# The second layer's normalised x turned by sixteen block transposes of VectorE instead of four of TensorE

## The chip, the core and the metric

The kernel runs on one core of one Trainium2 chip. What counts is the device time of one execution in microseconds, as the median of several runs. The engines are called by the names of the profile: PE (TensorE), ACT (ScalarE), DVE (VectorE), POOL (GpSimd) and SP (SyncE, which here only issues DMAs). Each engine works through its own queue in order.

## What is computed

Two layers over 8 sequences of 512 tokens with 128 features, all in fp32. Each layer adds an attention and a feed-forward part to x, both fed by the same layer norm of x:

```python
xn = _layernorm(x, axis=-1)
x = x + _L0_attn_ref(xn, ...) + _L0_ffn_ref(xn, ...)
xn = _layernorm(x, axis=-1)
x = x + _L1_attn_ref(xn, L1_attn_w_qkv, L1_attn_w_proj) + _L1_ffn_ref(xn, k0, k1, k2, s0, s1, s2)
```

The first layer's attention has 16 heads with two softmax maps each (differential attention); its feed-forward part is one product with x and the weights rounded in blocks of 32. The second layer's attention has 16 heads of 8 features with a rotary embedding. Its feed-forward part is three products with weights of +1 and -1 (128 to 512 to 512 to 128) with relu between them. So in the second layer xn feeds q, k and v, and the first feed-forward product.

## The kernel before

A sequence lies in x_all with its tokens on the 128 partitions, four per partition (T = 4), and 128 features behind each. Attention is computed in 24 units (ORDER): A and B are the two halves of the first layer's maps of a sequence, C is the second layer of one. A unit has 16 steps (STEPS). In each step PE makes four tiles of scores (`scores`, line 858), ACT takes their exponentials in two instructions (line 707), and PE multiplies the exponentials of two steps before with the values (`pv`, line 877). Between these, each step carries the jobs that the tables FIRST, LOOP and LAST list by hand for that unit and step: the norms, projections and feed-forward products of other sequences. LOOP is run for b = 2 to 5. Every engine walks through the same tables and does its own part of each item, so that a table's order is the order of all queues. A job of PE writes the one PSUM tile ps_misc, and DVE or ACT takes it out (TAKER); the next job waits for that.

The items around the change, for a sequence b:

- `norm1` parts 0 to 4 (`layer_norm`): DVE computes the layer norm of x; its last instruction (line 988) writes xn, with tokens on partitions.
- `x_t1`: PE waits for that, transposes four 128x128 tiles of xn into ps_misc (line 721), and DVE copies the result to xn_t (line 1135), which has features on partitions and the tokens in the free dimension, tile by tile (column 128 t + p). For b = 1 to 5 it is in step 14 of a unit C, and the norm's last part in step 12 (b = 1) or 13. In b = 0 and 6 it is in step 12, in b = 7 in step 11; there a `regroup` (DVE, lines 1318 and 1320) lies between norm and x_t1.
- `split_xn` (POOL): waits until xn_t has been taken, then rounds it to xn_hi (line 615) and computes xn_lo = xn_t - xn_hi (line 617).
- `ff0`, f = 0 to 3: PE waits for the split and multiplies xn_hi and xn_lo with the first feed-forward weights (lines 732 and 733); ACT applies the relu (line 657) and DVE splits the result (lines 1104 and 1106). The first comes in the step 0 of the unit after x_t1 for b = 1 to 5, two steps after x_t1 for b = 0 and 6, and four steps after it for b = 7.
- `q1`, `k1`, `v1`: PE waits for xn_t and multiplies it with the weights (line 728). q1 comes one step after x_t1 for b = 0, 6 and 7. For b = 1 to 4 it comes five steps after it and for b = 5 four, behind ff0.
- `take` (line 1308): DVE takes the products of eight steps out of ps_pv with block transposes; a following `pv` waits for it.

xn_hi and xn_lo lie in a part of the tiles of the second feed-forward stage (h1_hi, h1_lo), which `ff2_b` of the sequence before reads.

Of the kernel before, what the change touches and what calls it, by code (L numbers as in the profile page):

```python
# [18 lines left out]
T = N // P  # L19
# [39 lines left out]

TAKER = dict(x_t0="dve", x_t1="dve", q0="dve", k0="dve", v0="dve", q1="dve", k1="dve", v1="dve",  # L60
             qk_norm1="dve", w_t="dve", quant_t="dve", quant_mm="dve",
# [37 lines left out]
     15: [("ff_t", 0)]},  # L99
# [16 lines left out]
     9: [("take", -1, "C", 0), ("regroup", -1, "C", 0), ("project0", 0), ("norm1", 0, 0)], 11: [("norm1", 0, 1), ("norm1", 0, 2)],  # L116
     13: [("norm1", 0, 3), ("norm1", 0, 4)], 14: [("x_t1", 0)]},
]
# [99 lines left out]
def two_layers(nc, x_in, w_qkv0, w_proj0, b_proj0, lq1, lk1, lq2, lk2, subln, w_ffn0, b_ffn0,  # L218
               w_qkv1, w_proj1, k0, k1, k2, s0, s1, s2, rope, out):
    with ExitStack() as ctx:  # L220
# [21 lines left out]
        xn = sb("xn", [P, T, D], F32)  # L242
# [82 lines left out]
        first_written = [sem("first_written_q"), sem("first_written_k")]  # L325
        parts_written = [[sem(f"parts_written{layer}_{i}") for i in "qk"] for layer in range(2)]
        xn_split = sem("xn_split")
        ff_split = sem("ff_split")
# [121 lines left out]
        def load_shift(eng, U, half=None):  # L450
# [6 lines left out]
            for i in range(PARTS):  # L457
                if half is None:
                    eng.dma_start(q[ROWS[layer] + i::TILE_ROWS[layer], slot:slot + n].bitcast(F32),
                                  shift[h0:h0 + H, i, :].bitcast(F32)).then_inc(shift_loaded[U.stack], 16)  # L460
                    continue
                for g in range(TILES[layer]):
                    r, h = TILE_ROWS[layer] * g + ROWS[layer] + i, n * g + n // 2 * half
                    eng.dma_start(q[r:r + 1, n // 2 * half:n // 2 * (half + 1)].bitcast(F32),
                                  shift[h:h + n // 2, i, :].bitcast(F32)).then_inc(shift_loaded[group(U, half)], 16)

        def unit(kind, b):
# [114 lines left out]
        def _(pool):  # L582
# [28 lines left out]
            def split_xn(b):  # L611

                wait_taken(pool, ("x_t1", b))
                own_instruction(pool)
# [16 lines left out]
            def run(items):  # L631
                for name, b, *_ in items:
                    if name == "v_move":
                        move_values(b)
                    elif name == "x_t1":
                        split_xn(b)
# [81 lines left out]
        def _(pe):  # L718
# [16 lines left out]
            def job(item):  # L735
# [11 lines left out]
                if name == "w_t":  # L747
                    pe.wait_ge(setup_ops, SETUP_OPS - 2)
                    pe.wait_ge(quant_ops, 2 * QUANT_OPS)
                    ins = nc.tensor.transpose(ps[:, 0:P], quant[:, 0:P], ident[:])  # L750
                elif name in ("x_t0", "x_t1"):
                    pe.wait_ge(norm_ops[layer], (b + 1) * LN_OPS)
                    if item == ("x_t0", 0):

# [10 lines left out]
                elif name in ("q0", "k0", "q1", "k1"):  # L765
                    after("x_t" + name[1], b)
                    if item == ("q0", 0):
# [3 lines left out]
                elif name in ("v0", "v1"):  # L771
                    after("x_t" + name[1], b)
                    w = (w0_v if layer == 0 else w1_v)[:]
# [160 lines left out]
        def _(dve):  # L934
# [174 lines left out]
            def job(item):  # L1109
# [21 lines left out]
                elif item == ("x_t0", 0):  # L1131

                    taken(nc.vector.tensor_copy(xn_t[:, 0:N // 2], ps[:, 0:N // 2]))
                elif name in ("x_t0", "x_t1"):
                    taken(nc.vector.tensor_copy(xn_t[:], ps))  # L1135
# [168 lines left out]
            def take_pair(b, kind, pr):  # L1304
# [4 lines left out]
                last[:] = pv_taken, 2 * u + pr + 1  # L1309

            def regroup(b, kind, pr):

# [80 lines left out]
            def run(items):  # L1393
                for item in items:
# [20 lines left out]
                    elif name == "regroup":  # L1415
                        regroup(b, *args)
                    elif name in ("out_t0", "out_t1"):
                        turn_out(int(name[-1]), b)
# [62 lines left out]
```

## Time and profile before

| | us |
|---|---|
| median of 3 runs | 874.63 |
| lowest and highest | 871.47 and 875.64 |
| the profiled execution | 872.51 |
| its span, from first to last instruction | 870.7 |

All numbers of the trace are of that one execution. Busy times of an engine are the union of its instructions' times. In the timeline an instruction's row may stand for several like ones in a row (x4), and square brackets give how long the engine had been idle before it and which instruction ended that. Mean granted clock of TensorE over the span is 0.98 of full speed.

### The profile page before, as it was taken

Reading aid. Unit: us, or ns where it says so; the run is one execution under the profiler, and the core shown is the slowest. Engines: PE = TensorE matmul, PEld = TensorE weight load, DVE = VectorE, ACT = ScalarE, POOL = GpSimd, SP = SyncE. Lnnn points to the kernel's source line nnn. Section 1 sums busy time; section 2 is a strip of 40 time slices with the busy share of each in tenths; the row PEclk is TensorE's granted clock in tenths of the full one; section 3 lists DMA queues with packets and bytes.
Section 4 is the critical chain, followed back from the end, with each engine's and each line's share of the span. In section 5 each row is a group of like instructions: output and inputs, shape, how many; then the busy total and the mean of one; then the engine's idle time right before and its main releaser. Section 6 shows DMA issues by size and latency. Waiting matters only on the chain.

```text
span 870.7 us, 17841 instructions
## 1 busy us (share of the span) xinstructions
PE 808.3 (93%) x6767; PEld 287.7 (33%) x6767; DVE 545.4 (63%) x1205; ACT 765.2 (88%) x856; POOL 36.0 (4%) x57
## 2 busy tenths in 40 slices
PE   6688898999999989999999999999998999999995
PEld 4122222342333323333233323333242323333342
DVE  6667478676774666746775567756677476476321
ACT  3679997889889998999889998999988999889984
POOL 5000000000000000000000000000000000000000
PEclk9889998999999999999999999999999999999998
DMA  6807315630728015460527407281164704205100
GB/s 182 170 9 149 52 50 148 146 49 8 209 49 142 11 69 142 104 99 1 148 62 142 59 1 209 50 138 16 49 162 100 102 17 133 52 1 167 43 13 13
DMA packets 41618, 75.52 MB, mean 87 GB/s; under 512 B 5872, under 2 KB 7024, under 8 KB 41520
## 3 DMA queue, kind: packets, MB, share of 16 engines
q1 hardware_dynamic: 39612, 68.45, 36.1%
q0 software_dynamic: 1824, 5.70, 2.1%
q8 instruction: 57, 0.93, 0.5%
q14 instruction: 33, 0.27, 0.1%
q10 hardware_dynamic: 92, 0.16, 0.1%
HBM read 36.84 MB, written 35.65 MB: 83 GB/s over the span
## 4 chain that ended last, share of the span: by engine, by line
PE 72%; ACT 11%; DVE 9%; issue 5%; DMA 1%; DVEq 0%; SPq 0%; ACTq 0%; POOL 0%; POOLq 0%
PE ps_pv L877 31%; PE ps_s L858 20%; ACT probs L707 11%; PE ps_misc L728 7%; PE ps_misc L732 7%; PE ps_misc L733 5%; PE ps_misc L721 2%; DMA q_ab<-shift 1%; DVE pv_sb L1308 1%; DVE v_aug L1167 1%; DVE tmp L1159 0%; DVE h_lo L1106 0%; DVE tmp L1158 0%; PE ps_misc L779 0%; ACT ff_out L657 0%
## 5 line engine op out<-in xcount | busy, mean ns | idle before, releaser
L707 ACT ACTIVATE probs<-ps_s 128x1024 f32<-128x1024 f32 x768 | 726.5, 1046 | 61.8 <-PE ps_s L858 60.5
L877 PE MATMUL ps_pv<-probs,v_aug 128*32 128x512 f32 x3072 | 413.5, 610 | 10.2 <-ACT probs L707 5.8
L858 PE MATMUL ps_s<-q_ab,k_ab 18*128 18x512 f32 (+1 forms) x1088 | 143.5, 500 | 28.8 <-ACT probs L707 20.3
L858 PEld LDWEIGHTS ps_s<-q_ab,k_ab 18*128 18x128 f32 (+1 forms) x1088 | 54.7, 184 | 197.7 <-ACT probs L707 153.7
L877 PEld LDWEIGHTS ps_pv<-probs,v_aug 128*32 128x32 f32 x3072 | 61.9, 108 | 118.5 <-issue 81.2
L732 PE MATMUL ps_misc<-h_hi,k_w 128*128 128x512 f32 x192 | 85.7, 446 | 2.7 <-DVE v_aug L1167 1.2
L858 PE MATMUL ps_s<-q_c,k_c 34*128 34x512 f32 x448 | 84.8, 453 | 0.0
L1104 DVE CAST h_hi<-ff_out 128x512 fp32r<-128x512 f32 x64 | 27.4, 428 | 89.0 <-ACT ff_out L657 87.5
L1308 DVE STREAM_TRANSPOSE pv_sb<-ps_pv 128x512 f32<-128x512 f32 x48 | 34.4, 717 | 70.8 <-PE ps_pv L877 67.5
L733 PE MATMUL ps_misc<-h_lo,k_w 128*128 128x512 f32 x192 | 75.9, 395 | 0.0
L732 PEld LDWEIGHTS ps_misc<-h_hi,k_w 128*128 128x128 f32 x192 | 35.9, 187 | 88.4 <-issue 48.8
L858 PEld LDWEIGHTS ps_s<-q_c,k_c 34*128 34x128 f32 x448 | 36.1, 184 | 74.7 <-ACT probs L707 60.2
L657 ACT ACTIVATE ff_out<-ps_misc 128x512 f32<-128x512 f32 x64 | 39.1, 610 | 17.9 <-PE ps_misc L733 13.8
L1106 DVE TENSOR_TENSOR h_lo<-ff_out,h_hi 128x512 fp32r<-128x512 f32 x64 | 44.3, 692 | 2.2
L733 PEld LDWEIGHTS ps_misc<-h_lo,k_w 128*128 128x128 f32 x192 | 36.1, 188 | 4.3
L1191 DVE TENSOR_TENSOR x_all<-ps_misc,x_all 128x512 f32<-128x512 f32 x24 | 16.6, 692 | 26.3 <-PE ps_misc L721 12.8
L728 PE MATMUL ps_misc<-xn_t,w_qk 128*32 128x512 f32 x248 | 32.3, 592 | 0.0
L1167 DVE COPY v_aug<-ps_misc 128x512 f32<-128x512 f32 x14 | 9.7, 692 | 27.5 <-PE ps_misc L728 27.1
L615 POOL CAST h_hi<-xn_t 128x512 fp32r<-128x512 f32 x8 | 4.9, 608 | 502.9 <-DVE xn_t L1135 502.9
L1320 DVE TENSOR_TENSOR heads<-pv_sb,recip 128x256 f32<-128x256 f32 x48 | 20.4, 425 | 1.7
L728 PE MATMUL ps_misc<-wp,quant_t 128*32 128x128 f32 x512 | 17.8, 282 | 2.7 <-DVE quant_t L1327 2.7
L728 PEld LDWEIGHTS ps_misc<-wp,quant_t 128*32 128x32 f32 x512 | 15.2, 113 | 12.8 <-issue 11.3
(164 smaller groups left out, 563.1 us busy)
## 6 DMA issues: line engine op xcount, KB each, us to landing
parts_dram<-qk_parts SPq DMA_DIRECT2D x32, 512.0 KB, 3.7
parts_dram<-qk_parts SPq DMA_DIRECT2D x62, 256.0 KB, 4.1
q_ab<-parts_dram SPq DMA_DIRECT2D x60, 128.0 KB, 4.6
k_ab<-parts_dram SPq DMA_DIRECT2D x60, 128.0 KB, 5.9
q_c<-parts_dram SPq DMA_DIRECT2D x14, 512.0 KB, 7.5
k_c<-parts_dram SPq DMA_DIRECT2D x14, 512.0 KB, 8.8
out_dram<-x_all POOLq DMA_DIRECT2D x8, 256.0 KB, 6.8
x_all<-in_L_attn_x_dram POOLq DMA_DIRECT2D x7, 256.0 KB, 6.1
```

Source lines behind the costliest of these rows:

```text
L657: nc.scalar.activation(ff_out[:], ps_misc[:], ACT.Relu).then_inc(job_taken_act, 1)
L707: nc.scalar.activation(probs[:, U.slot(s), 2 * half:2 * half + 2], ps_s[:, 2 * pair:2 * pair + 2], ACT.Exp, scale=SCALE[U.layer]).then_inc ...
L728: ins = nc.tensor.matmul(ps[c, :], w[:, c], x, start=True, stop=True)
L732: nc.tensor.matmul(ps, w, hi, start=start, stop=False)
L733: return nc.tensor.matmul(ps, w, lo, start=False, stop=stop)
L858: ins = nc.tensor.matmul(ps_s[:, bank, :], k[row:row + n, slot, c * P:(c + 1) * P], q[row:row + n, slot, :], start=True, stop=True)
L877: ins = nc.tensor.matmul(ps_pv[32 * j:32 * j + 32, :], v_aug[:, U.v, c, a:a + 32], probs[:, U.slot(s), j, :], start=c == 0 and not odd, st ...
L1104: nc.vector.tensor_copy(hi, ff_out[:]).then_inc(ff_split, 1)
L1106: nc.vector.tensor_tensor(lo, ff_out[:], hi.bitcast(F32), ALU.subtract).then_inc(ff_split, 1)
L1167: taken(nc.vector.tensor_copy(own_values(unit("C" if layer else "A", b).v), ps.rearrange("p (t h e) -> p t h e", t=T, h=H)))
L1308: nc.vector.transpose(pv_sb[:], ps_pv[:]).then_inc(pv_taken, 1)
L1320: nc.vector.tensor_tensor(dst, v[:, :, :, 0:HD], rows(recip[:], HD), ALU.mult).then_inc(regroup_ops, 1)
```

## The change

The job x_t1 goes. In its place in the tables stand the two parts of `turn1`. In each part DVE issues eight block transposes. Each takes 32 of xn's partitions (tokens), all four t and 32 features: four blocks of 32x32, which it turns and writes to the 32 rows of xn_t that belong to these features. A source of 32 partitions a is written to four targets f, so that sixteen instructions fill xn_t. Each increments a new semaphore, turned[1]; the readers of xn_t in PE (q1, k1, v1) and in POOL (split_xn) wait for its count of 16 per sequence. split_xn now also waits for ff2_b of the sequence before, which the queue of jobs had implied. PE has no part in the turning any more, and ps_misc isn't used for it. The first layer's x is turned as before (x_t0). The diff, without two of the tables' hunks that read like the others:

```diff
@@ -57,7 +57,7 @@
 INDEX = {unit: u for u, unit in enumerate(ORDER)}
 
 
-TAKER = dict(x_t0="dve", x_t1="dve", q0="dve", k0="dve", v0="dve", q1="dve", k1="dve", v1="dve",
+TAKER = dict(x_t0="dve", q0="dve", k0="dve", v0="dve", q1="dve", k1="dve", v1="dve",
              qk_norm1="dve", w_t="dve", quant_t="dve", quant_mm="dve",
              project0="dve", project1="dve", ff0="act", ff1="act", ff1_b="act", ff2="act", ff2_b="act", ff_t="dve",
              fast="dve")
@@ -84,7 +84,7 @@
     {1: [("take", 0, "B", 1), ("regroup", 0, "B", 1), ("combine", 0, 0)], 3: [("combine", 0, 1), ("combine", 0, 2)],
      4: [("combine", 0, 3)], 5: [("combine", 0, 4), ("combine", 0, 5)], 6: [("out_t0", 0), ("project0", 0), ("norm1", 0, 0)],
      8: [("norm1", 0, 1)], 9: [("take", 1, "A", 0), ("norm1", 0, 2), ("norm1", 0, 3)], 11: [("norm1", 0, 4), ("regroup", 1, "A", 0)],
-     12: [("x_t1", 0)], 13: [("q1", 0)], 14: [("rope", 0, "q", 0), ("ff0", 0, 0)], 15: [("rope", 0, "q", 1), ("k1", 0)]},
+     12: [("turn1", 0, 0), ("turn1", 0, 1)], 13: [("q1", 0)], 14: [("rope", 0, "q", 0), ("ff0", 0, 0)], 15: [("rope", 0, "q", 1), ("k1", 0)]},
     {0: [("take", 1, "A", 1), ("rope", 0, "k", 0)], 2: [("rope", 0, "k", 1), ("ff0", 0, 1)],
      3: [("qk_norm1", 0), ("norm0", 2, 0), ("norm0", 2, 1)], 4: [("v1", 0)], 5: [("exact1", 0)],
      6: [("ff0", 0, 2), ("norm0", 2, 2), ("ff0", 0, 3)], 7: [("norm0", 2, 3)], 8: [("norm0", 2, 4), ("x_t0", 2)],
@@ -95,7 +95,7 @@
      3: [("quant_t", 2), ("bias", 2), ("combine", 1, 0), ("combine", 1, 1), ("combine", 1, 2)], 4: [("quant_mm", 2)],
      5: [("combine", 1, 3)], 6: [("ff1", 0, 3), ("combine", 1, 4), ("ff1_b", 0, 3)], 7: [("exact0", 2), ("combine", 1, 5)],
      8: [("v0", 2)], 9: [("take", 0, "C", 0), ("out_t0", 1)], 10: [("regroup", 0, "C", 0), ("project0", 1), ("norm1", 1, 0)],
-     11: [("norm1", 1, 1), ("norm1", 1, 2), ("norm1", 1, 3)], 12: [("norm1", 1, 4), ("ff2", 0), ("ff2_b", 0)], 14: [("x_t1", 1)],
+     11: [("norm1", 1, 1), ("norm1", 1, 2), ("norm1", 1, 3)], 12: [("norm1", 1, 4), ("ff2", 0), ("ff2_b", 0)], 14: [("turn1", 1, 0), ("turn1", 1, 1)],
      15: [("ff_t", 0)]},
 ]
 
@@ -114,7 +114,7 @@
     {1: [("take", 0, "B", 1), ("ff_t", -1)], 2: [("regroup", 0, "B", 1)], 3: [("combine", 0, 0)], 4: [("v0", 1), ("combine", 0, 1)],
      5: [("combine", 0, 2), ("combine", 0, 3)], 7: [("combine", 0, 4), ("combine", 0, 5)], 8: [("out_t0", 0)],
      9: [("take", -1, "C", 0), ("regroup", -1, "C", 0), ("project0", 0), ("norm1", 0, 0)], 11: [("norm1", 0, 1), ("norm1", 0, 2)],
-     13: [("norm1", 0, 3), ("norm1", 0, 4)], 14: [("x_t1", 0)]},
+     13: [("norm1", 0, 3), ("norm1", 0, 4)], 14: [("turn1", 0, 0), ("turn1", 0, 1)]},
 ]
 
 LAST = [
...
...
@@ -324,6 +324,7 @@
         bound0_ops = sem("bound0_ops")
         first_written = [sem("first_written_q"), sem("first_written_k")]
         parts_written = [[sem(f"parts_written{layer}_{i}") for i in "qk"] for layer in range(2)]
+        turned = [sem("turned0"), sem("turned1")]
         xn_split = sem("xn_split")
         ff_split = sem("ff_split")
         v_moved = sem("v_moved")
@@ -464,6 +465,13 @@
                     eng.dma_start(q[r:r + 1, n // 2 * half:n // 2 * (half + 1)].bitcast(F32),
                                   shift[h:h + n // 2, i, :].bitcast(F32)).then_inc(shift_loaded[group(U, half)], 16)
 
+        def wait_turned(eng, layer, b):
+
+            if layer == 0:
+                wait_taken(eng, ("x_t0", b))
+            else:
+                eng.wait_ge(turned[layer], 16 * (b + layer))
+
         def unit(kind, b):
             return Unit(INDEX[kind, b])
 
@@ -610,7 +618,10 @@
 
             def split_xn(b):
 
-                wait_taken(pool, ("x_t1", b))
+                wait_turned(pool, 1, b)
+                if b > 0:
+
+                    wait_taken(pool, ("ff2_b", b - 1))
                 own_instruction(pool)
                 nc.gpsimd.tensor_copy(xn_hi, xn_t[:]).then_inc(xn_split, 1)
                 pool.wait_ge(xn_split, 2 * b + 1)
@@ -629,10 +640,10 @@
                 nc.gpsimd.tensor_copy(own_values(unit("C", b).v), x_all[:, b - 5].rearrange("p t (h e) -> p t h e", h=H)).then_inc(v_moved, 1)
 
             def run(items):
-                for name, b, *_ in items:
+                for name, b, *args in items:
                     if name == "v_move":
                         move_values(b)
-                    elif name == "x_t1":
+                    elif name == "turn1" and args[0] == 1:
                         split_xn(b)
                     elif name == "project1":
                         store(b)
@@ -748,9 +759,9 @@
                     pe.wait_ge(setup_ops, SETUP_OPS - 2)
                     pe.wait_ge(quant_ops, 2 * QUANT_OPS)
                     ins = nc.tensor.transpose(ps[:, 0:P], quant[:, 0:P], ident[:])
-                elif name in ("x_t0", "x_t1"):
-                    pe.wait_ge(norm_ops[layer], (b + 1) * LN_OPS)
-                    if item == ("x_t0", 0):
+                elif name == "x_t0":
+                    pe.wait_ge(norm_ops[0], (b + 1) * LN_OPS)
+                    if b == 0:
 
                         for t in range(T):
                             ins = nc.tensor.transpose((ps if t < T // 2 else ps_s[:, 1, :])[:, t * P:(t + 1) * P], xn[:, t, :], ident[:])
@@ -763,13 +774,13 @@
                     pe.wait_ge(fast_w_made, n + 1)
                     ins = in_columns(ps, fast_w[:, n * P:(n + 1) * P], xn_t[:])
                 elif name in ("q0", "k0", "q1", "k1"):
-                    after("x_t" + name[1], b)
+                    wait_turned(pe, layer, b)
                     if item == ("q0", 0):
                         pe.wait_ge(w0_made, 4)
                     w = (w0_qk if layer == 0 else w1_qk)[:, 0 if name[0] == "q" else 1, :]
                     ins = in_columns(ps, w, xn_t[:])
                 elif name in ("v0", "v1"):
-                    after("x_t" + name[1], b)
+                    wait_turned(pe, layer, b)
                     w = (w0_v if layer == 0 else w1_v)[:]
                     for t in range(T):
                         ins = in_columns(ps[:, t * P:(t + 1) * P], xn_t[:, t * P:(t + 1) * P], w)
@@ -1131,7 +1142,7 @@
                 elif item == ("x_t0", 0):
 
                     taken(nc.vector.tensor_copy(xn_t[:, 0:N // 2], ps[:, 0:N // 2]))
-                elif name in ("x_t0", "x_t1"):
+                elif name == "x_t0":
                     taken(nc.vector.tensor_copy(xn_t[:], ps))
                 elif name == "quant_t":
                     taken(nc.vector.tensor_copy(quant_t[:], ps))
@@ -1308,6 +1319,15 @@
                 nc.vector.transpose(pv_sb[:], ps_pv[:]).then_inc(pv_taken, 1)
                 last[:] = pv_taken, 2 * u + pr + 1
 
+            def turn(layer, b, part):
+
+                settled()
+                for a in (2 * part, 2 * part + 1):
+                    for f in range(4):
+                        dst = xn_t[32 * f:32 * f + 32].rearrange("p (t a c) -> p a t c", t=T, a=4)[:, a]
+                        nc.vector.transpose(dst, xn[32 * a:32 * a + 32, :, 32 * f:32 * f + 32]).then_inc(turned[layer], 1)
+                last[:] = turned[layer], 16 * (b + layer - 1) + 8 * (part + 1)
+
             def regroup(b, kind, pr):
 
                 G = 2 * INDEX[kind, b] + pr
@@ -1414,6 +1434,8 @@
                         take_pair(b, *args)
                     elif name == "regroup":
                         regroup(b, *args)
+                    elif name in ("turn0", "turn1"):
+                        turn(int(name[-1]), b, *args)
                     elif name in ("out_t0", "out_t1"):
                         turn_out(int(name[-1]), b)
                     elif name == "bound0":
```

## Rows read from the trace of the kernel before

**Rows 1.** The page, part 1: span, and busy time of the engines
```profile
span 870.7 us, 17841 instructions
...
PE 808.3 (93%) x6767; PEld 287.7 (33%) x6767; DVE 545.4 (63%) x1205; ACT 765.2 (88%) x856; POOL 36.0 (4%) x57
```

**Rows 2.** Groups by line and form, DVE: busy us, mean ns | idle before
```profile
L1327 DVE STREAM_TRANSPOSE quant_t<-heads 128x512 f32<-128x512 f32 x8 | 5.7, 712 | 0.3
L1327 DVE STREAM_TRANSPOSE quant_t<-quant 128x512 f32<-128x512 f32 x8 | 5.7, 711 | 0.3
...
L1179 DVE STREAM_TRANSPOSE norm_row<-norm_ok 32x32 f32<-32x32 f32 x8 | 1.6, 199 | 0.4 <-DVE norm_ok L1177 0.2
```

**Rows 3.** Timeline of DVE: start us, us, instruction; dependent pair, then independent pair
```profile
196.01 0.16 DVE L952 TENSOR_TENSOR stat<-stat 128x4 f32<-128x4 f32 x1
196.20 0.16 DVE L954 SCALAR_TENSOR_TENSOR stat<-stat 128x4 f32<-128x4 f32 x1
...
32.10 0.28 DVE L1363 TENSOR_TENSOR bias<-bias 128x128 f32<-128x128 f32 x1
32.30 0.28 DVE L1364 TENSOR_SCALAR wp<-wp,sub_col 128x128 f32<-128x128 f32 x1
```

**Rows 4.** Timeline of all engines around the turn of b = 2
```profile
301.42 0.69 DVE L988 TENSOR_TENSOR xn<-tmp,stat 128x512 f32<-128x512 f32 x1
...
302.63 0.66 PE L721 MATMUL ps_misc<-ident,xn 128*128 128x128 f32 x4
...
303.32 0.69 DVE L1135 COPY xn_t<-ps_misc 128x512 f32<-128x512 f32 x1 [1.21 <-PE ps_misc L721]
...
304.88 1.27 POOL L617 TENSOR_TENSOR h_lo<-xn_t,h_hi 128x512 fp32r<-128x512 f32 x1
...
306.42 0.50 PE L732 MATMUL ps_misc<-h_hi,k_w 128*128 128x512 f32 x1
306.75 0.40 PE L733 MATMUL ps_misc<-h_lo,k_w 128*128 128x512 f32 x1
...
307.45 0.63 ACT L657 ACTIVATE ff_out<-ps_misc 128x512 f32<-128x512 f32 x1
```

**Rows 5.** Busy time: stretch, us, PE, PEld, DVE, ACT, POOL, clock, DMA
```profile
294.70:314.00 19.30, 18.63 (x138) 5.56 (x136) 11.07 (x29) 19.30 (x22) 1.88 (x2) 1.00 0.01 1
```

**Rows 6.** Timeline at b = 1, 0, 6 and 7: last work before, first reader
```profile
197.86 0.69 DVE L988 TENSOR_TENSOR xn<-tmp,stat 128x512 f32<-128x512 f32 x1
...
204.20 0.50 PE L732 MATMUL ps_misc<-h_hi,k_w 128*128 128x512 f32 x1
...
116.77 0.43 DVE L1320 TENSOR_TENSOR heads<-pv_sb,recip 128x256 f32<-128x256 f32 x1
...
119.92 1.04 PE L728 MATMUL ps_misc<-xn_t,w_qk 128*32 128x512 f32 x8
...
709.69 0.43 DVE L1320 TENSOR_TENSOR heads<-pv_sb,recip 128x256 f32<-128x256 f32 x1
...
711.29 1.04 PE L728 MATMUL ps_misc<-xn_t,w_qk 128*32 128x512 f32 x8
...
778.14 0.42 DVE L1320 TENSOR_TENSOR heads<-pv_sb,recip 128x256 f32<-128x256 f32 x1
...
780.74 1.04 PE L728 MATMUL ps_misc<-xn_t,w_qk 128*32 128x512 f32 x8
```

**Rows 7.** Timeline of PE at two stalls; busy time (as Rows 5) behind them
```profile
140.05 0.50 PE L732 MATMUL ps_misc<-h_hi,k_w 128*128 128x512 f32 x1 [1.16 <-DVE v_aug L1167]
...
671.19 1.77 PE L877 MATMUL ps_pv<-probs,v_aug 128*32 128x512 f32 x8 [1.93 <-DVE pv_sb L1308]
...
671.42:674.83 3.41, 3.41 (x20) 0.69 (x16) 0.43 (x2) 1.07 (x3) 0.00 (x0) 0.50 0.94 235
142.35:149.17 6.82, 6.59 (x32) 1.70 (x28) 4.96 (x17) 4.37 (x5) 0.00 (x0) 0.50 0.50 108
```

4 rows, old and new, of the table LAST are left out of this document.

## The prediction

> **What bounds the kernel now.** I read the page first [rows 1]: TensorE (PE) is busy 808.3 of 870.7 us, ScalarE (ACT) 765.2, VectorE (DVE) 545.4. So two engines are nearly full, and VectorE has room on average. That average is not what decides here: all queues are in order, and what counts is when a result of VectorE is wanted by TensorE. The second view is the groups of instructions by line [rows 2], with prices of block transposes. The third is the timeline around the eight places where the second layer's x is turned, one for each sequence b; a unit there is sixteen steps, and in each step TensorE makes the scores, then the products of the step before last, then the jobs of the table. The fourth is the busy time by stretches, which shows the granted clock.
>
> At b = 2 [rows 4] the timeline reads: the layer norm's last instruction (L988) ends at 302.11. TensorE comes to the four transposes at 302.63, VectorE copies xn_t at 303.32 to 304.01, GpSimd (POOL) ends its split of it at 304.88 + 1.27 = 306.15, and TensorE reads the split in the first ff0 matmul at 306.42, in the middle of a queue without a gap. From the end of the norm to that read are 4.31 us, of which GpSimd takes 2.14 from the end of the copy to the end of its split. So VectorE has 302.11 to about 304.1 to deliver xn_t, 2.0 us, before TensorE has to stand still. b = 3, 4 and 5 repeat this pattern.
>
> **What goes.** Per sequence four transposes, and one copy of 0.69 us. The four transposes are one merged row of 0.66 us [rows 4], so TensorE gets back at most 8 x 0.66 = 5.3 us in all. I cost it at zero in b = 2 to 5: ScalarE is busy in 19.30 of the 19.30 us from 294.7 to 314.0 [rows 5], so a TensorE that is 0.66 us earlier meets a ScalarE that is not. In b = 0, 1, 6, 7 it would be worth up to 0.66 us each, if TensorE did not then wait for xn_t; below it does, so the gain is swallowed there as well.
>
> **What comes.** Sixteen STREAM_TRANSPOSE instructions of 32 partitions x 128 elements, one behind the other with no wait between those of one part. No row of before has this form. One alone is bounded well: 32x32 elements take 199 ns and 128x512 take 711 ns [rows 2], a slope of (711 - 199) / 480 = 1.07 ns per element, so 128 elements take 199 + 96 x 1.07 = 301 ns. The period is what is unknown:
> - Upper end, as if each waited for the one before: small dependent instructions start 0.19 to 0.20 us apart at 0.16 us each (L952, L954), some 0.035 us beyond the duration [rows 3]. Period 0.336, sixteen take 5.4 us.
> - Lower end, as independent instructions of 128 elements do: L1363 and L1364 start 0.20 us apart, though each lasts 0.28 [rows 3]. Fifteen periods of 0.20 and one duration, 3.3 us.
> - Far end, elements alone with nothing between them: 15 x 128 x 1.07 ns + 0.30 = 2.4 us.
>
> I take 5.4 us. The rows that overlap all stay on partitions 0 to 127 from one instruction to the next; here every instruction writes another group of 32 partitions than the one in front of it, and the nearest row in form, the 32x32 block transpose of 199 ns, is followed by nothing that overlaps it. The Trainium skill, page "VectorE: DVE Perf Modes", section "Two Vector instructions with no wait between them", says it as a rule: an instruction whose output starts in another quadrant than the last output is held until every earlier one has finished. By that rule all sixteen are held and the sum is the one at 5.4 us; without it, the one at 3.3 us. No row of before tells which. The same page of the Trainium skill, section "Rules for kernel authors", sends a whole 128x128 transpose to TensorE where PSUM will do as its target, which speaks against this change; no row of before compares the two.
>
> **Who waits.** The copy ends after one further instruction; now xn_t is ready 5.4 us after VectorE is free. At each site the first reader in TensorE's queue stands still, and behind it stand scores and products; ScalarE then runs dry.
> - b = 2: 302.11 + 5.4 = 307.5; GpSimd ends 2.14 later, 309.65; ff0 starts at 309.7 for 306.42, TensorE 3.3 late. ScalarE's relu came at 307.45 [rows 4]; it can't start before the job's second matmul ends, 306.75 + 0.40 - 306.42 = 0.73 us after ff0's start, so at 310.45. ScalarE is 3.0 late. Both engines being late, I charge 3.0. Four such: 12.0.
> - b = 1: norm ends 198.55, xn_t at 203.95, split at 206.1; ff0 for 204.20 at 206.15, TensorE 1.95 late. ScalarE takes some 0.3 of it as above; charge 1.7 [rows 6].
> - b = 0: here a regroup (L1320, ends 117.19) lies between norm and turn, and q1 follows one step on. xn_t at 122.6, q1 for 119.92 at 122.7: 2.8. The split is then ready before ff0 [rows 6].
> - b = 6: regroup ends 710.12, xn_t 715.5, q1 for 711.29 at 715.6: 4.3. b = 7: 778.56, 784.0, 784.05 for 780.74: 3.3 [rows 6].
>
> Sum 12.0 + 1.7 + 2.8 + 4.3 + 3.3 = 24.1 us. VectorE's own addition, 8 x (5.4 - 0.7) = 38 us, costs nothing beyond this: its next work at b = 2 is the split of the relu's result (L1104), and the relu came at 307.45 [rows 4], about when the turn ends. GpSimd's two new waits are for the turn itself and for ff2_b of the sequence before, long done in the table; behind them its queue holds only stores and value moves. SyncE's loads shift with the rope results, by no more than all else.
>
> **What the stalls do to the clock.** TensorE idles 1.93 us before 671.19, and from 671.42 to 674.83 it is granted 0.50, the 1.2 GHz level, while busy all the 3.41 us [rows 7]; half of its work of that time, 1.7 us, is lost. An idle time of 1.16 us before 140.05 is followed by 6.82 us at 0.50 from 142.35 [rows 7]. The eight new stalls are 1.9 to 4.3 us, at or above those that the low level followed. Some of the low stretch may lie in the stall itself. I charge 1.5 us each, 12 us; the ends are 0 and 2.5 each.
>
> **Sum.** 872.5 (the profiled execution, span 870.7) + 24.1 + 12 = 908.6 us. The median of the three runs is 2.1 us above the profiled one; I say 908.
>
> **Rivals.**
> 1. The instructions overlap, 3.3 us per turn. Stalls: b = 2 to 5 1.0 each at ScalarE (split ends 302.11 + 3.3 + 2.14 = 307.55, relu at 308.4), b = 0 0.7, b = 1 none, b = 6 2.2, b = 7 1.2: 8.1 us, and the low clock behind one or two of them, 1.6 to 3. Time 882 to 884. For it: L1363/L1364. Against: they don't change partitions.
> 2. Turns as in the forecast, but the stalls leave the clock alone, since they fall differently: 872.5 + 24.1 = 896.6, or 892 to 900. Against it: the two places above, with idle times no longer than these.
> 3. The other side: short turns. At 2.4 us only b = 6 and 7 stall (1.3, 0.3), b = 0 and 1 gain as much; no change. From 2.0 us per turn downward nothing waits in b = 2 to 5, and TensorE's 0.66 us count in b = 0, 1, 6, 7 at most: 4 x 0.66 = 2.6 us faster, 870. It needs a period of 0.11 us, below the 128 elements of 1.07 ns.
> 4. The change doesn't take TensorE's part away: excluded by the diff, since no job x_t1 is left.
>
> **How the numbers follow.** Forecast with low clock 0.62, rival 2 0.13, rival 1 0.16, rival 3 0.04 faster and 0.04 no change, 0.01 else. The forecast's own range is 900 to 917 (stalls 22 to 27 us by a turn of 5.1 to 5.8, clock 5 to 18). Including rival 2 and most of rival 1 gives 882 to 917. A measurement of this kernel tells about 0.5%, 4.4 us, from no change; rivals 1 and 2 lie above it. So faster 0.04, same 0.05, slower 0.91.
>
> **What would show it.** Right: sixteen rows of about 0.30 us in each turn, 0.33 to 0.34 apart, GpSimd's L615 waiting for them, ff0 waiting for GpSimd by about 3 us at b = 2 to 5 and q1 waiting for the turn at b = 0, 6, 7; the granted clock at 0.5 behind these. Wrong: periods near 0.20 (rival 1), TensorE waits of 3 us with a clock that stays (rival 2), or first reads that find xn_t ready (rival 3). The forecast fails most easily in the period of the transposes and in what a stall costs beyond its own length.

## The result: 5.7% slower, and what the profile after shows

The changed kernel takes 923.17 us (median of 4 runs, 916.92 to 926.62), the kernel before 873.86 us in the runs beside it; the ratio is 1.0567, 95% interval 1.0522 to 1.0611. The forecast was 908 us with a range of 882 to 917. The direction was right, the size was not: +49 us measured, +34 us forecast. The profiled execution took 923.29 us, its span is 921.5 us, and the mean granted clock of TensorE over it is 0.947, where it was 0.98.

From the page after, the lines that answer to [rows 1], and two groups of part 5 (line, engine, operation, busy us, mean ns of one, idle before and what ended it):

```profile
span 921.5 us, 17881 instructions
...
PE 831.1 (90%) x6735; PEld 288.6 (31%) x6735; DVE 578.6 (63%) x1325; ACT 767.4 (83%) x856; POOL 35.8 (4%) x57
...
L1328 DVE STREAM_TRANSPOSE xn_t<-xn 32x128 f32<-32x128 f32 x128 | 38.7, 303 | 4.1
L626 POOL CAST h_hi<-xn_t 128x512 fp32r<-128x512 f32 x8 | 4.9, 607 | 534.6 <-DVE xn_t L1328 534.6
```

A page read by busy shares alone would mislead here: DVE's share is 63% before and after, although it has 33 us more to do, and PE is *busier*, 831.1 for 808.3 us, although 32 transposes have gone. PE has more busy time with less work because it spends more of it at the lower clock, as the stretches below and the run with filled waits show.

The waits of PE (who waited for whom, us in total, times, longest) name the new stalls:

```profile
PE ps_misc L743 <- POOL h_lo L628: 15.9, 5, 3.5
PE ps_misc L739 <- DVE xn_t L1328: 11.0, 3, 4.5
PE ps_s L869 <- DMA q_ab<-shift: 9.5, 2, 7.1
```

The first is ff0 waiting for the split at b = 1 to 5, the second q1 waiting for the turn at b = 0, 6 and 7: 26.9 us. The forecast had PE late by 1.95 + 4 x 3.3 = 15.2 us at the first and 10.4 us at the second, 25.6 together. The timeline at b = 2 answers to [rows 4]:

```profile
310.07 0.69 DVE L999 TENSOR_TENSOR xn<-tmp,stat 128x512 f32<-128x512 f32 x1
...
310.80 5.32 DVE L1328 STREAM_TRANSPOSE xn_t<-xn 32x128 f32<-32x128 f32 x16
...
317.00 1.25 POOL L628 TENSOR_TENSOR h_lo<-xn_t,h_hi 128x512 fp32r<-128x512 f32 x1
318.41 0.58 PE L743 MATMUL ps_misc<-h_hi,k_w 128*128 128x512 f32 x1 [3.29 <-POOL h_lo L628]
...
319.45 0.60 ACT L668 ACTIVATE ff_out<-ps_misc 128x512 f32<-128x512 f32 x1 [3.23 <-PE ps_misc L744]
320.07 1.94 PE L888 MATMUL ps_pv<-probs,v_aug 128*32 128x512 f32 x8
```

Sixteen transposes take 5.32 us, (5.32 - 0.30) / 15 = 0.335 us from start to start; ff0 stands 3.29 us. All of that is as forecast. The last line is what was not priced in full: a group of products takes 1.94 us where it takes 1.06 to 1.07 us at full clock. The busy time by stretches shows the low level (1.2 GHz, 0.50) behind each of the eight stalls; here are b = 2 and 3, which differ (columns as in [rows 5]):

```profile
318.62:322.03 3.41, 3.41 (x15) 0.64 (x14) 1.12 (x2) 2.39 (x3) 0.00 (x0) 0.50 0.01 2
424.43:434.67 10.24, 9.86 (x40) 2.68 (x44) 3.74 (x7) 6.57 (x8) 0.23 (x1) 0.50 0.01 2
```

The low stretches at the eight turns last 3.41 us at b = 0, 1 and 2, 10.24 us at b = 3, 4, 5 and 7, and 6.83 us at b = 6: 58 us in all. PE is busy in 55 of them, at half speed, so some 28 us of its work are lost there by this estimate. The charge had been 1.5 us each, 12 in all.

### The profile page after: what moved, and what is told of

The parts are those of the page before. It is cut to its first block, busy times and chain, and to the rows that moved or that the text cites. A ratio compares the mean times of both kernels' runs of the same rounds, so it can differ in the third digit from the quotient of the medians.

```text
span 921.5 us, 17881 instructions
## 1 busy us (share of the span) xinstructions
PE 831.1 (90%) x6735; PEld 288.6 (31%) x6735; DVE 578.6 (63%) x1325; ACT 767.4 (83%) x856; POOL 35.8 (4%) x57
## 4 chain that ended last, share of the span: by engine, by line
PE 64%; DVE 17%; ACT 9%; issue 5%; DMA 2%; POOL 1%; SPq 1%; DVEq 0%; ACTq 0%; POOLq 0%
PE ps_pv L888 28%; PE ps_s L869 17%; ACT probs L718 8%; PE ps_misc L739 7%; PE ps_misc L743 7%; PE ps_misc L744 5%; DVE xn_t L1328 4%; PE ps_misc L732 1%; DMA q_ab<-shift 1%; DVE pv_sb L1319 1%; DVE tmp L990 1%; POOL h_lo L628 1%; DVE xn L999 1%; DVE stat L992 1%; DVE stat L963 1%
## 5 line engine op out<-in xcount | busy, mean ns | idle before, releaser
L888 PE MATMUL ps_pv<-probs,v_aug 128*32 128x512 f32 x3072 | 426.9, 629 | 7.7 <-ACT probs L718 3.8
L869 PE MATMUL ps_s<-q_ab,k_ab 18*128 18x512 f32 (+1 forms) x1088 | 148.2, 518 | 32.4 <-ACT probs L718 22.7
L743 PE MATMUL ps_misc<-h_hi,k_w 128*128 128x512 f32 x192 | 88.7, 462 | 18.1 <-POOL h_lo L628 15.9
L744 PE MATMUL ps_misc<-h_lo,k_w 128*128 128x512 f32 x192 | 78.5, 409 | 0.0
L739 PE MATMUL ps_misc<-xn_t,w_qk 128*32 128x512 f32 x248 | 36.6, 666 | 11.0 <-DVE xn_t L1328 11.0
L1328 DVE STREAM_TRANSPOSE xn_t<-xn 32x128 f32<-32x128 f32 x128 | 38.7, 303 | 4.1
L1202 DVE TENSOR_TENSOR x_all<-ps_misc,x_all 128x512 f32<-128x512 f32 x24 | 16.6, 692 | 24.1 <-PE ps_misc L739 11.3
L1169 DVE TENSOR_TENSOR tmp<-ps_misc,trig 128x512 f32<-128x512 f32 x16 | 11.1, 692 | 21.8 <-PE ps_misc L739 21.2
```

Source lines behind the costliest of these rows:

```text
L739: ins = nc.tensor.matmul(ps[c, :], w[:, c], x, start=True, stop=True)
L743: nc.tensor.matmul(ps, w, hi, start=start, stop=False)
L744: return nc.tensor.matmul(ps, w, lo, start=False, stop=stop)
L869: ins = nc.tensor.matmul(ps_s[:, bank, :], k[row:row + n, slot, c * P:(c + 1) * P], q[row:row + n, slot, :], start=True, stop=True)
L888: ins = nc.tensor.matmul(ps_pv[32 * j:32 * j + 32, :], v_aug[:, U.v, c, a:a + 32], probs[:, U.slot(s), j, :], start=c == 0 and not odd, st ...
L1328: nc.vector.transpose(dst, xn[32 * a:32 * a + 32, :, 32 * f:32 * f + 32]).then_inc(turned[layer], 1)
```

## Experiments

Three questions were open: does the period of 0.335 us come from the change of partitions, are the stalls the whole of the loss or does something else add to it, and what is DVE's turn worth where nobody waits for it. All ratios are to the kernel before, run beside each. A trace is of one execution, and where its time isn't the run's median, the text says so.

**Same group of partitions.** Each transpose writes to the group of 32 partitions that it reads, so that xn_t is then not the transposed x:

```diff
-                        dst = xn_t[32 * f:32 * f + 32].rearrange("p (t a c) -> p a t c", t=T, a=4)[:, a]
+                        dst = xn_t[32 * a:32 * a + 32].rearrange("p (t a c) -> p a t c", t=T, a=4)[:, f]
```

> The sixteen transposes of a turn read the same elements as in the changed kernel, but each writes the 32 rows of xn_t that carry the same partition numbers as its source, in another block of columns. So xn_t is not the transposed x, and the second layer computes with wrong operands; sizes and instructions are the same. Four transposes in a row keep source and target partitions. Theory (an instruction waits for the earlier ones when it changes its group of 32 partitions): starts within a group of four 0.20 us apart, 0.34 between groups, a turn of 3.8 us in place of 5.4; waits of PE at the eight turns fall from 26.9 us to about 14, and the time lands at 895 to 905. Rival (block transposes never overlap, whatever they touch): starts stay 0.34 apart, the time stays at 917 to 927.

Measured in one run: 894.7 us. The turn at b = 2, in the timeline of DVE:

```profile
308.00 3.63 DVE L1328 STREAM_TRANSPOSE xn_t<-xn 32x128 f32<-32x128 f32 x16
```

3.63 us in place of 5.32. In a group of four the starts are 0.235, 0.193 and 0.193 us apart, and 0.29 where the group changes; the median transpose shows 260 ns in place of 303. So block transposes do overlap when they stay on their partitions, and the rival falls. PE waits 7.5 + 6.0 = 13.5 us at the turns, about 14 had been expected; the time is just below the 895 to 905 expected.

**Targets kept, sources changed.** The turn as in the changed kernel, with the loops exchanged:

```diff
-                for a in (2 * part, 2 * part + 1):
-                    for f in range(4):
+                for f in (2 * part, 2 * part + 1):
+                    for a in range(4):
```

> The same sixteen transposes in another order: the target group is the outer loop, so that four in a row write the same 32 partitions and only the source group changes. Theory (a change of the source's group holds an instruction as well as one of the target's): starts stay 0.34 apart, turn 5.4 us, time 917 to 927. Rival (only a change of the target's group holds it): twelve of sixteen starts are 0.20 apart, turn 3.8 us, time 895 to 905.

Measured: 924.5 us in one run, and the same turn as in the changed kernel:

```profile
310.24 5.31 DVE L1328 STREAM_TRANSPOSE xn_t<-xn 32x128 f32<-32x128 f32 x16
```

Keeping the target alone brings nothing: with the source's group changed, each instruction starts 0.33 us or more behind the one before, whose own time is 0.30 us. A turn by whole 32-partition pieces can't avoid both, since each pair of source and target occurs once.

**The waits filled with matmuls.** The useless work goes into PE's queue ahead of the wait, so that PE waits as long for the same thing but doesn't stand still (and likewise ahead of q1 for b = 0, 6 and 7):

```diff
+FILLERS = (3, 2, 3, 3, 3, 3, 4, 4)
...
+                    if f == 0 and b in (1, 2, 3, 4, 5):
+                        for _ in range(FILLERS[b]):
+                            in_columns(ps, wp1[:], trig[:, 0, :])
                     pe.wait_ge(xn_split, 2 * (b + 1))
```

> The changed kernel, with matmuls of no use (fp32, four of 32 columns by 512, about 0.9 us a group) put into PE's queue ahead of each of the eight waits: three groups at b = 0, 2, 3, 4, 5, two at b = 1, four at b = 6 and 7. The waits keep their end, PE does not stand still. Theory (the 22 to 25 us that the change costs beyond the waits themselves are PE at half clock behind them): granted clock back to 0.98, time 923 - 22 = 898 to 903. Rival (the rest comes from somewhere else, such as later results of DVE): the time stays within 3 us of 923, or grows by what the fillers take.

Measured: 898.35 us (4 runs), ratio 1.0293 (1.024 to 1.0347), mean granted clock 0.982. Timeline at b = 2, then the busy time of the 10.24 us behind the wait at b = 3:

```profile
311.35 2.76 PE L740 MATMUL ps_misc<-trig,wp 128*32 128x512 f32 x24
...
314.74 0.50 PE L744 MATMUL ps_misc<-h_hi,k_w 128*128 128x512 f32 x1 [0.63 <-POOL h_lo L629]
...
315.84 1.06 PE L895 MATMUL ps_pv<-probs,v_aug 128*32 128x512 f32 x8
...
419.80:430.04 10.24, 9.86 (x74) 2.92 (x74) 6.70 (x13) 9.28 (x12) 0.00 (x0) 1.00 0.01 2
```

ff0 comes as late behind the norm as in the changed kernel without fillers (7.6 us behind its end in both), but the clock is 1.00 behind it and the products take 1.06 us. This run splits the loss. By the medians 898.4 - 873.9 = 24.5 us (25.6 by the ratio) are the stalls themselves, for which the forecast was 24.1 us, and the 923.2 - 898.4 = 24.8 us that come back with the fillers are the rest. The four runs spread from 896.3 to 903.9, and the interval of the ratio leaves 21 to 30 us for the stalls and 19 to 28 for the rest.

The starts of ACT's exponentials, compared step by step between the profiled executions (872.5, 896.6 and 923.3 us), say where the two parts lie. The stalls add 24.4 us at the eight turns in the filled kernel. Without the fillers another 26.7 us are lost, all of it at these places to 0.2 us:

| Place | low stretch, us | lost beyond the filled kernel, us |
|---|---|---|
| b = 0, 1, 2 | 3.41 each | 1.5, 0.8, 1.3 |
| b = 6 | 6.83 | 2.7 |
| b = 3, 4, 5, 7 | 10.24 each | 4.0, 3.9, 4.2, 4.0 |
| start of unit A of b = 7 | 6.83, behind a DMA wait | 2.9 |
| the first units, ahead of any turn | | 1.5 |

So some 22.5 us are the clock behind the eight stalls. The other 4.4 us come back with the fillers too, but not at the turns.

**DVE's part alone.** The kernel before with the sixteen transposes added ahead of its own copy:

```diff
+                if name == "x_t1":
+                    settled()
+                    for a in range(4):
+                        for f in range(4):
+                            dst = xn_t[32 * f:32 * f + 32].rearrange("p (t a c) -> p a t c", t=T, a=4)[:, a]
+                            nc.vector.transpose(dst, xn[32 * a:32 * a + 32, :, 32 * f:32 * f + 32]).then_inc(turned, 1)
+                    last[:] = turned, 16 * (b + 1)
                 dve.wait_ge(job_made, PLAN.made[item])
```

> The kernel before with the sixteen transposes of DVE added ahead of its own copy of xn_t: PE still transposes, DVE's copy overwrites the turned x with the same values. Readers wait for the copy. This does DVE's part alone. Theory (only the time at which xn_t is ready counts): each wait of PE is that of the changed kernel plus 0.73 us for the copy, 26.9 + 8 x 0.73 = 32.7 us, and as much clock loss behind them: 923 + 6 = 929, 925 to 934. Rival (PE's part gone, and not DVE's length, is what lets the clock fall and the kernel slow down): below 900.

Measured: 928.61 us (4 runs), ratio 1.0647 (1.0613 to 1.0681). With PE's transposes in place the kernel loses what the changed one loses, and a little more for the copy, 5.4 us for the 6 expected. PE waits 16.5 us for POOL at b = 2 to 5, 12.2 us for DVE at b = 0, 6 and 7, and at b = 1 2.5 us one job earlier, at the transposes of the feed-forward result, which follow in ps_misc: 31.2 us for the 32.7 expected. The trace is of the fastest of the four executions, 923.22 us at a clock of 0.959; the other three took 928.5 to 932.3 at 0.944 to 0.946. The loss is in the time at which xn_t is ready, and not in TensorE's missing part.

**TensorE's part gone, at next to no price.** Two of a turn's sixteen transposes; fourteen of the sixteen blocks of xn_t are left out:

```diff
-                for a in (2 * part, 2 * part + 1):
-                    for f in range(4):
+                for a in (2 * part,):
+                    for f in (0,):
...
-                        nc.vector.transpose(dst, xn[...]).then_inc(turned[layer], 1)
+                        nc.vector.transpose(dst, xn[...]).then_inc(turned[layer], 8)
```

> The changed kernel with one transpose per part in place of eight, so two of the sixteen of a turn; fourteen of the sixteen blocks of xn_t keep an older sequence's values, and the second layer computes with them. All else runs as in the changed kernel. This leaves PE's part gone and takes DVE's price away: the turn takes 0.7 us. Theory: nothing waits, granted clock 0.98, and since ACT sets the pace around the turns of b = 2 to 5 only b = 0, 1, 6 and 7 may gain, up to 0.6 each: 870.5 to 874. Rival (PE bounds everywhere, as its 93% busy says): 8 x 0.66 = 5 us, 868 to 869.

Measured: 871.97 us (12 runs), ratio 0.9982 (0.9964 to 1.0000), so 1.6 us won, with an interval that just reaches no change, of at most 5.3 us that TensorE no longer spends. In b = 2 to 5 PE begins the scores behind the transposes 0.6 us earlier than in the kernel before, and is back at the old place one step on: ACT sets the pace there, as [rows 5] said. Even a turn at next to no price would have brought 0.2%.

**Readers later.** First for b = 1 to 5 alone, in the changed kernel and in the kernel before:

```diff
-    {0: [("ff0", -1, 0)], 1: [("take", -2, "C", 1), ("ff0", -1, 1)], 2: [("regroup", -2, "C", 1)], 3: [("q1", -1)],
-     4: [("rope", -1, "q", 0), ("ff0", -1, 2)], 5: [("out_t1", -2), ("rope", -1, "q", 1)], 6: [("k1", -1)],
-     7: [("rope", -1, "k", 0), ("rope", -1, "k", 1)], 9:
+    {1: [("take", -2, "C", 1)], 2: [("regroup", -2, "C", 1), ("ff0", -1, 0)], 3: [("q1", -1)],
+     4: [("rope", -1, "q", 0), ("ff0", -1, 1)], 5: [("out_t1", -2), ("rope", -1, "q", 1)], 6: [("k1", -1)],
+     7: [("rope", -1, "k", 0), ("rope", -1, "k", 1), ("ff0", -1, 2)], 9:
...
```

For b = 5 the table LAST is changed likewise; there q1, k1 and their rotations move by a step too.

> The changed kernel, with ff0 0, 1 and 2 of b = 1 to 5 two to three steps later in the tables (steps 2, 4 and 7 of the A unit in place of 0, 1 and 4), so that the split is ready when PE comes to it. Theory (stall and clock behind it are the whole cost): waits of PE for POOL go from 15.9 us to 0, the five places give back what the step times show there, 3.6 + 4.3 + 7.0 + 7.0 + 7.2 = 29 us, so the time is about 894, 890 to 899, with 11 us of waits left at b = 0, 6 and 7. Rival (DVE's added 38 us weigh on their own): less than half of that comes back, over 908.

> Control for the run before: the kernel before, turned by PE, with the same later ff0 0, 1 and 2 for b = 1 to 5. If the move of these jobs has a price or a gain of its own, it shows here. Theory: PE and ACT are both full in this stretch, the jobs only change places; 872 to 878 us. If it is below 870, the gain found by moving them in the changed kernel was partly the move's own.

Measured: 891.98 us for the changed kernel (4 runs, ratio 1.0200, 1.0164 to 1.0236) and 876.02 us for the one before (10 runs, ratio 1.0031, 1.0015 to 1.0047). The wait of PE for POOL is gone, and with it 31 of the 49 us. In the traces the changed kernel is 3.2 us behind the other at the start of unit A of b = 2, and 3.1 us behind it at step 10 of unit B of b = 6: the turns of b = 2 to 5 between them, and b = 1's first reader, now cost nothing. What is left between the two, 16.0 us, lies mainly at b = 0, 6 and 7, where q1 still waits:

```profile
PE ps_misc L739 <- DVE xn_t L1328: 11.0, 3, 4.5
```

Then all eight, with q1 and its followers two to three steps later for b = 0, 6 and 7; here b = 6 in the control:

```diff
-     13: [("q1", 6)], 14: [("rope", 6, "q", 0), ("rope", 6, "q", 1), ("ff0", 6, 0)], 15: [("k1", 6)]},
-    {0: [("take", 7, "A", 1), ("regroup", 7, "A", 1)], 1: [("v1", 6)], 2: [("rope", 6, "k", 0), ("ff0", 6, 1)],
+     15: [("q1", 6)]},
+    {0: [("take", 7, "A", 1), ("regroup", 7, "A", 1), ("rope", 6, "q", 0), ("ff0", 6, 0)], 1: [("rope", 6, "q", 1), ("k1", 6)],
+     2: [("rope", 6, "k", 0), ("ff0", 6, 1)], 3: [("v1", 6)],
```

> The changed kernel with every first reader moved behind the turn: ff0 of b = 1 to 5 as in the run before, and q1 with its followers two steps later for b = 7, two to three for b = 0 and 6. Theory (the waits and the clock behind them are the whole cost, DVE's 38 us are free): PE waits 0 to 1 us at the eight turns, granted clock 0.98, the time 892 less 4.2 + 7.0 + 7.3 from the step times there = 873, 868 to 877; and a gain of up to 0.66 us per sequence from PE's part gone, if anywhere, would bring it to 868. Rival: DVE's longer way delays its later work, and the time stays over 880.

> Control: the kernel before with the tables of the run with all readers later. Theory: 872 to 878. The difference to that run is what the turn by DVE costs or brings where nobody waits for it; I expect the run by DVE to be 0 to 3 us faster, since PE is free of 8 x 0.66 us and in most places ACT sets the pace.

Measured: 892.27 us (5 runs, ratio 1.0216) and 892.66 us for the control (5 runs, ratio 1.0221). The 873 us of the expectation were missed by 19 us, and the control shows why: my table has a price of its own. Of the control's waits of PE, and in its timeline the k1 of b = 6 and the ff0 behind it:

```profile
PE ps_misc L734 <- DVE tmp L1161: 12.1, 7, 5.3
```

```profile
730.75 1.04 PE L730 MATMUL ps_misc<-xn_t,w_qk 128*32 128x512 f32 x8
...
738.56 0.80 PE L734 MATMUL ps_misc<-h_hi,k_w 128*128 128x512 f32 x1 [5.34 <-DVE tmp L1161]
```

At b = 0 and 6 I had put the second ff0 one step behind k1, whose result DVE takes only after other work, and PE stands before that ff0 for 4.5 and 5.3 us. The comparison still answers its question for b = 1 to 5: from the start of unit A of b = 2 to step 10 of unit B of b = 6 the distance between the two traces stays at 1.3 to 1.4 us. There nobody waits for the sixteen transposes, and DVE's longer work costs nothing and brings nothing. That the whole times agree to 0.4 us proves less: the control has a DMA wait of 3.85 us at the start of unit A of b = 7 that the other run lacks, and at b = 0 and 6 both stand still for other reasons.

**TensorE's old waits filled.** The kernel before, with fillers at five of its own waits, and then at three:

```diff
+            def fill(ps, n):
+                for _ in range(n):
+                    in_columns(ps, ident, xn[:].rearrange("p t d -> p (t d)"))
...
                         if s == 0:
+                            fill(ps_s[:, 0, :], 6)
                             wait_taken(pe, ("fast", 0, "k", 0))
```

> The kernel before, untouched but for matmuls of no use in PE's own five long waits: six groups (about 0.9 us each) before the first scores, four before the first transposes of quant, one before ff0 2 of b = 0, two before the ninth product step of unit B of b = 6, two before the last projection. Theory (a wait of PE costs half of its work for some time behind it, wherever it comes from): the low stretches behind 24.3, 44.8, 140, 671 and 862.5 go; 1.5 + 1.5 + 2.4 + 1.6 + 0.9 = 8 us, time 864 to 870, granted clock above 0.99. Rival (the clock falls for another reason than PE standing still, such as the DMAs running then): clock and time stay.

> The kernel before with the useless matmuls at three of the five places only: seven groups before the first scores, four before the first transposes of quant, two before the last projection. The place in unit B of b = 6 is left as it was, since in the run with all five the loads of the next unit came late there and took back 4.8 us. Theory: the 2.5 us won in the first unit and 0.9 us in the last stay, 874 - 3 = 871, 869 to 872. Rival (what PE wins early is always lost at that load again): 873 to 877.

With five: 876.89 us (9 runs), ratio 1.0044 (1.0026 to 1.0062), where 864 to 870 had been expected. With three (seven groups in place of six at the first): 871.69 us (12 runs), ratio 0.9981 (0.9967 to 0.9995), as expected. With five the median clock is 0.987, above the 0.98 of the kernel before, and the kernel is still slower, so a higher mean clock is not in itself time won. The traced execution is the best of the nine: 873.22 us at a clock of 0.994, the time of the kernel before; the other eight took 876.2 to 878.8 at 0.984 to 0.989, and no trace shows where their clock fell. In the traced one no low stretch is left at the first four places, which speaks for PE's standing still as what the clock fell for, and PE is 3.2 us ahead up to unit B of b = 6. Then the loads for unit A of b = 7 have not landed when PE comes to them, and a longer wait of PE with the low level behind it takes back 4.8 us. The same scores in the kernel before, and in this run:

```profile
684.31 0.51 PE L858 MATMUL ps_s<-q_ab,k_ab 18*128 18x512 f32 x4 [0.49 <-DMA q_ab<-shift]
```

```profile
683.15 0.80 PE L864 MATMUL ps_s<-q_ab,k_ab 18*128 18x512 f32 x4 [4.15 <-DMA q_ab<-shift]
```

The kernel before waits there too, but for 0.49 us; its low stretch of [rows 7] lay ahead of the same loads. The loads don't keep pace with PE: from the first of the DMAs issued ahead of these scores to the scores 15.6 us pass in the kernel before and 17.6 us here. The run with three fillers leaves that place alone and is 0.2% faster than the kernel before. It isn't a clean test of that place, since it leaves out the filler at b = 0 as well, and the filler at b = 6 also brings a wait for ps_misc with it.

## Why the forecast had the right sign and the wrong size

- **What bounds the kernel, and that b = 2 to 5 gain nothing from TensorE's part**: right. At next to no price for DVE the whole gain is 1.8 us by the medians; the bound in rival 3 was 2.6 us.
- **Duration and period of a transpose**: 301 ns and 0.336 us forecast, 303 ns and 0.335 us measured. The choice of the upper end was right, and the reason too: the experiment with kept partitions brings 0.19 to 0.24 us, the exchange of loops nothing. The prediction named the half of the rule that speaks of the output; the same section of the Trainium skill (page "VectorE: DVE Perf Modes", section "Two Vector instructions with no wait between them") holds an instruction in the same way when its input starts in another quadrant than the first input of the last one. The traces agree in all three cases: changed target 0.335, changed source 0.33 to 0.34, both kept 0.19 to 0.24 us. Rival 1 falls. The 38 us added to DVE come out as 37 us (8 x 5.32 less 5.5 us of copies); its busy time grows by 33 us only, since the short gaps between the transposes aren't busy.
- **Who waits, and the sum of 24.1 us**: right. PE's waits are 26.9 us for 25.6, and the run with the waits filled costs 24.5 us by the medians and 24.4 us by the steps at the turns.
- **What the stalls do to the clock**: this step failed. "I charge 1.5 us each, 12 us" stands for 22.5 us at the eight turns by the steps, 2.8 us each, and for 24.8 us by the medians with all that came back with the fillers. The price came from the one stretch of 3.41 us behind 671.19 in [rows 7], and for stretches of that length it holds: 0.8 to 1.5 us at b = 0, 1 and 2. What failed is that every stretch was taken to be that short. The other row of the same group, 6.82 us behind a shorter stall, was cited and didn't enter the charge; here five of the eight are 6.83 or 10.24 us long and cost 2.7 to 4.2 us, above the stated upper end of 2.5.
- **The second-order term**: PE's wait for the DMA at the start of unit A of b = 7 grows from 0.49 to 2.40 us, with 6.83 us of low clock behind it, and costs 2.9 us. The prediction had "SyncE's loads shift with the rope results, by no more than all else". It is small, but it is a wait that grows where the low stretch ahead of it has gone away.
- **The upper end of the range**, 917 us, is the profiled execution with 27 us of stalls and 18 us of clock, although the prediction's own ends of 0 and 2.5 us for a stall give 20 us of clock. The measured 923.17 lies 6 us above it, by the clock term again. That the direction was right is no luck, since the stalls alone, forecast at 24.1 us, make the kernel slower by more than the noise.

**Open:** why stalls of nearly equal length (3.29 us at b = 2, 3.34 us at b = 3) are followed by 3.41 us in one place and 10.24 us in the next. It is not the place: in the run with the targets kept, whose stalls are the same to 0.02 us, b = 2 has 10.24 us behind it, b = 7 has 3.41 us, and the 2.45 us stall at b = 1 has no low stretch at all. In the run with the same group, where a stall is 1.6 to 1.8 us at b = 2 to 5, b = 3 has 10.24 us, b = 4 has 3.41 us and the other two none. One thing goes with the length in the traces with stalls at the turns (these two, the changed kernel, DVE's part alone, and the later readers of b = 1 to 5). Seven stretches began after the stall had ended, as here at b = 2 (318.62 for 318.41), and all seven are 3.41 us long. Eighteen began 0.2 us or more before its end, as at b = 3 (424.43 for 424.81), and are 6.83 or 10.24 us long; three began 0.1 us or less before it and are 3.41 us. No run varied that on purpose, so it is a pattern and not a cause.

## What to carry to other kernels

An engine with 37% idle time is not a free place to move work to: what counts is the distance in time between the result and its first reader in an in-order queue, here 2.0 us for a step that went from one instruction to 5.3 us. If TensorE has to stand still for microseconds, price the stall twice: the waits here cost some 25 us and the low clock behind them nearly as much again, 22.5 us at the turns, and useless matmuls in the waits gave that half back. And when a clock or a wait is mended at one place, look at the next DMA that was hidden behind it.

## What the runs showed of the hardware that I had not expected

- Block transposes of 32x128 elements that keep source and target partitions start 0.19 to 0.24 us apart at some 260 ns each; with either group changed they start 0.33 to 0.34 us apart at 303 ns.
- A stall of 3.3 us was followed by up to 10.24 us at the 1.2 GHz level with TensorE busy for 9.86 of them, so the low level lasts on while TensorE works. With 2.76 us of the wait filled, 0.63 us of idle time was followed by none. The same stall at the same place had a low stretch of 3.41 us behind it in one execution and of 10.24 us in another, and a stall of 2.5 us had one of 3.41 us in one and none in the other.
- A mean granted clock of 0.987 (median of nine runs) in place of 0.98 went with a kernel 0.4% slower. In the one traced execution, at 0.994 and no faster than the kernel before, 3.2 us gained early were lost at a load that came only 1.2 us earlier than in the kernel before, while PE came to it 4.8 us earlier.
